# An attention edge stage on one core: products by edge, weighting on DVE, selections on ScalarE

## What is computed

```
ms = src_s[edge_src] + dst_s[edge_dst]           # 64 scalars
mv = src_v[edge_src] + dst_v[edge_dst]           # 32 vectors of 3
w1..w5 = split(h @ rw3 + roff)                   # 224 weights
Y1 = sqrt(3) * edge_vec / |edge_vec|
ds = [w1*ms, w4*(mv . Y1)/sqrt(3)]
dv = [(w2*ms) Y1, w3*mv, w5*cross(mv, Y1)/sqrt(2)]
ls, lv = ds @ lin_ws + lin_bs, einsum(dv, lin_wv)
alpha, vs, vv = ls[:, :64], ls[:, 64:], lv       # 8 heads
a = softmax over the edges of one destination of
    sum_k smooth_leaky(alpha) * alpha_dot
ns = segment_sum(vs * a);  nv = segment_sum(vv * a)
```

## Time and profile before

| | us |
|---|---|
| runs, median of 3 | 9831.51 (9822.02 to 9844.67) |
| the profiled execution | 9813.87 |
| its span | 9812.0 |
| the second edge stage, first to last step on DVE | 5344.8 to 9028.0 |

### The profile page before, as it was taken

How to read it: one execution, slowest core, us unless ns; L and a number is a source line. 1 busy time by engine, 2 the same in 40 slices (tenths; PEclk the granted TensorE clock), 3 DMA queues, 4 the chain that set the end, 5 groups by cost and what they waited for, 6 DMA issues and landing times. The chain is left out here.

```text
span 9812.0 us, 193495 instructions
## 1 busy us (share of the span) xinstructions
PE 8373.1 (85%) x35878; PEld 5079.2 (52%) x35878; DVE 7735.9 (79%) x14864; ACT 4874.4 (50%) x9073; POOL 7372.6 (75%) x4571
## 2 busy tenths in 40 slices
PE   0788888888888869999985999999999999998588
PEld 0444444444444422222222777777777777777233
DVE  3177777777777768888886999999999999998465
ACT  0176666666666631121121555555555555555355
POOL 4378888888888878778774888888888888886331
PEclk9599999999999989999997999999999999999799
DMA  5578888888888877778773666666666666665222
GB/s 208 180 161 167 167 168 166 167 167 167 167 167 167 167 213 275 267 271 282 264 270 109 136 137 144 137 143 137 144 138 144 138 142 137 144 137 122 59 70 52
DMA packets 1235170, 1618.04 MB, mean 165 GB/s; under 512 B 222610, under 2 KB 1010589, under 8 KB 1178973
## 3 DMA queue, kind: packets, MB, share of 16 engines
q1 hardware_dynamic: 758950, 1273.86, 40.0%
q0 software_dynamic: 475584, 338.58, 27.1%
HBM read 1533.79 MB, written 444.07 MB: 202 GB/s over the span
## 5 line engine op out<-in xcount | busy, mean ns | idle before, releaser
L1952 POOL DMA_INDIRECT e_m<-TS,e_at x1568 | 2631.8, 1678 | 583.7 <-issue 461.4
L442 POOL DMA_INDIRECT sums<-e_total,e_place x1568 | 2506.9, 1599 | 565.9 <-DMA sums<-e_total,e_place 314.5
L579 PE MATMUL ps<-e_win,e_pick 128*128 128x448 f32 x3136 | 1325.8, 568 | 165.0 <-DVE e_u L476 97.0
L579 PEld LDWEIGHTS ps<-e_win,e_pick 128*128 128x128 f32 x3136 | 612.5, 201 | 921.6 <-issue 864.1
L2275 ACT ACTIVATE e_dT<-ps 128x512 f32<-128x512 f32 x1176 | 660.0, 596 | 495.5 <-PE ps L2149 340.1
L2275 ACT ACTIVATE e_oT<-ps 128x512 f32<-128x512 f32 x784 | 468.9, 598 | 615.1 <-PE ps L2177 373.2
L742 DVE SCALAR_TENSOR_TENSOR r_y<-ps,w_rb,r_rstd 128x512 f32<-128x512 f32 x394 | 295.6, 750 | 579.9 <-issue 533.2
L1096 POOL TENSOR_TENSOR n_zv<-n_zv,n_ast 128x1536 f32<-128x1536 f32 x200 | 703.6, 3518 | 36.6 <-DMA n_zv<-in_x_groups 22.5
L1936 POOL TENSOR_TENSOR e_val<-e_val 128x640 f32<-128x640 f32 x392 | 670.9, 1712 | 61.9 <-ACT e_val L2252 61.9
L2018 DVE TENSOR_TENSOR e_q<-e_row,dstI 128x512 f32<-128x512 int32 x392 | 704.2, 1796 | 13.3 <-PE ps L2163 13.3
L711 PE MATMUL ps<-r_sq,w_avg 128*128 128x512 f32 x788 | 458.1, 666 | 277.4 <-issue 277.4
(11 more groups left out here) (448 smaller groups left out, 19299.8 us busy)
## 6 DMA issues: line engine op xcount, KB each, us to landing
e_win<-T SPq DMA_DIRECT2D x1568, 168.0 KB
n_z<-in_x_groups SPq DMA_DIRECT2D x400, 512.0 KB
n_zv<-in_x_groups SPq DMA_DIRECT2D x800, 192.0 KB
TOT<-e_tot SPq DMA_DIRECT2D x392, 352.0 KB, 2.6
e_row<-in_src_rows SPq DMA_DIRECT2D x98, 1024.0 KB
e_local<-LR SPq DMA_DIRECT2D x196, 512.0 KB
e_row<-in_dst_rows SPq DMA_DIRECT2D x98, 1024.0 KB
e_win<-TD SPq DMA_DIRECT2D x1568, 60.0 KB
```

Source lines behind the costliest of these rows:

```text
L442: pool.indirect_dma_start(sums[c], bass.IndirectOffsetOnAxis(ap=place[:, r % 4, c:c + 1], axis=0), total[:, r % 4, c, 0:MSG0], None, compu ...
L579: pe.matmul(g[:, c, :], pick[:, p, R * c:R * c + R], win[:, s, c, :], start=True, stop=True).then_inc(spread, 1)
L1952: pool.indirect_dma_start(m_[:, r % 4, c, :], None, TS, bass.IndirectOffsetOnAxis(ap=at[:, gp, col:col + 1], axis=0), compute_op=ALU.add). ...
```

## The change

- **Maps by edge.** `map_scalars` and `map_vectors` take the turned piece as the stationary operand, tile by tile (four products of 128 columns instead of one of 512), so that edges come out on the partitions. The two copies to `oT` and `turn_back` go. Scalars go to bank 4, vectors to bank 5. `map_scalars` waits for ScalarE's `outs` and DVE's `silued` of the step before.
- **Weighting.** `weighted` goes from POOL to DVE, at the beginning of a step, seven behind instead of eight. `totals`, `keep_totals` and `store` go from six to seven behind. `members` is as it was.
- **Selections.** `selections` goes from DVE to ScalarE, as relu(1 - |x - own number|) in two activations.
- **Directions for the heads.** ScalarE repeats `yx` into `ye`, 96 numbers, and one product on DVE with it takes the place of three.
- **Order.** `tops_down` stands before the turns, ScalarE's `results` in the same step, `shift` after `weigh`.

```diff
@@ vector: body
                         more = not (isinstance(t, int) and t == PASSES - 1 and r == STEPS - 1)
+                        if not i.before(7):
+                            weighted(i)
                         if more:
                             sums(after)
                         if r % 4 == 1 and not i.before(5):
                             scans(i)
-                        if i.plus(4).within():
-                            selections(i.plus(4))
                         if not i.before(1):
                             results(i.plus(-1))
+                        if more:
+                            weigh(after)
                         if r % 4 == 1 and not i.before(5):
                             shift(i)
-                        if more:
-                            weigh(after)
                         if not i.before(5):
                             members(i)
@@ vector: results
                     dve.wait_ge(outs, i.n(2, 2))
-                    for x in range(3):
-                        last = dve.tensor_tensor(
-                            turn_by_y[:, :, 4 * x:4 * x + 4].rearrange("r (c h) j -> r c h j", c=GT),
-                            vectors4[:, :, :, 12:16], bc(bc(yx[:, x, bass.ds(i.n(4), GT)], HEADS, 2), 4, 3), ALU.mult)
-                    last.then_inc(by_y, 1)
...
+                    dve.wait_ge(mapped, i.n(2, 2))
+                    y3 = ye[:, p].rearrange("r (c h) i -> r (c h) i", c=GT)
+                    dve.tensor_tensor(turn_by_y[:].rearrange("r a (i j) -> r a i j", i=3),
+                                      bc(vector_out4.rearrange("r c (h x) -> r (c h) x", x=16)[:, :, 12:16], 3, 2),
+                                      bc(y3, 4, 3), ALU.mult).then_inc(by_y, 1)
@@ tensor: totals, map_scalars, map_vectors
-                    j = i.r - 6
+                    j = i.r - 7
...
                     gate(pe, k)
-                    pe.wait_ge(kept, i.n(5, 2))
-                    pe.matmul(ps[:, bank(i, 5), :], W["la"][:].rearrange("u a h x -> u (a h x)"), dT[:, 0, :], start=True, stop=True
-                              ).then_inc(turned, 1)
+                    pe.wait_ge(kept, i.n(3, 1))
+                    if not i.before(1):
+                        gate(pe, k)
+                        pe.wait_ge(outs, i.n(2))
+                        gate(pe, k)
+                        pe.wait_ge(silued, i.n(2, -1))
+                    for c in range(GT):
+                        last = pe.matmul(scalar_out4[:, c], dT[:, 0, R * c:R * c + R],
+                                         W["la"][:].rearrange("u a h x -> u (a h x)"), start=True, stop=True)
+                    last.then_inc(mapped, 1)
...
+                    pe.wait_ge(kept, i.n(3, 3))
+                    if not i.before(1):
                         gate(pe, k)
                         pe.wait_ge(freed, i.n(1))
                     for c in range(GT):
-                        last = pe.transpose(out4[:, c, 128 * j:128 * j + 128], oT[:, j, R * c:R * c + R], I[:])
+                        pe.matmul(vector_out4[:, c], dT[:, 1, R * c:R * c + R], W["lb"][:].rearrange("u h x -> u (h x)"),
+                                  start=True, stop=False)
+                        last = pe.matmul(vector_out4[:, c], dT[:, 2, R * c:R * c + R],
+                                         W["lc"][:].rearrange("u h x -> u (h x)"), start=False, stop=True)
                     last.then_inc(mapped, 1)
@@ scalar: selections
+                    act.activation(pick[:, p, :], local[:, gp, GT * R * s:GT * R * s + GT * R], ACT.Abs, bias=minus[:, 0:1]
+                                   ).then_inc(distant, 1)
+                    gate(act, k)
+                    act.wait_ge(distant, i.n(1, 1))
+                    act.activation(pick[:, p, :], pick[:, p, :], ACT.Relu, bias=one[:, 0:1], scale=-1.0).then_inc(picked, 1)
@@ scalar: body
+                        if r % 4 == 2 and not i.before(6):
+                            weigh_up(i.plus(-1))
                         keep(i, 0)
                         keep(i, 1)
-                        if not i.before(6):
-                            keep_totals(i, 0)
+                        if i.plus(4).within():
+                            selections(i.plus(4))
                         keep(i, 2)
-                        keep(i, 3)
-                        if not i.before(6):
+                        results(i)
+                        if not i.before(7):
+                            keep_totals(i, 0)
                             keep_totals(i, 1)
-                        if r % 4 == 1 and not i.before(5):
-                            weigh_up(i)
-                        keep(i, 4)
```

More of the change, by code:

```diff
@@ L1921, in _ @@
                 passes(sp, body)
-                for r in range(6):
-                    store(At(PASSES, r), 6)
+                for r in range(7):
+                    store(At(PASSES, r), 7)
                 for s in range(STEPS):
@@ L2100, in _ @@
                 dve.wait_ge(ones_set, 2)
-                for r in range(4):
-                    selections(At(0, r))
                 sums(At(0, 0))
@@ L2109, in _ @@
                 for r in range(5):
+                    weighted(At(PASSES, r))
                     members(At(PASSES, r))
+                for r in range(5, 7):
+                    weighted(At(PASSES, r))
             @block.tensor
@@ L2219, in body @@
                         turn(i, 1)
-                        if not i.before(6):
+                        map_scalars(i)
+                        turn(i, 2)
+                        if not i.before(7):
                             totals(i, 0)
-                        turn(i, 2)
-                        if r % 4 == 1 and not i.before(5):
-                            tops_down(i)
-                        map_scalars(i)
-                        if not i.before(6):
+                        map_vectors(i)
+                        if not i.before(7):
                             totals(i, 1)
-                        map_vectors(i)
                         if r % 4 == 0 and not i.before(4):
@@ L2306, in body @@
                             keep_far(i.plus(3), 1, far2(i, 1))
[L2307 to L2308 removed]
+                        if r % 4 == 2 and not i.before(6):
+                            weigh_up(i.plus(-1))
                         keep(i, 0)
                         keep(i, 1)
[L2311 removed]
+                        if i.plus(4).within():
+                            selections(i.plus(4))
+                        keep(i, 2)
+                        results(i)
+                        if not i.before(7):
                             keep_totals(i, 0)
[L2313 to L2315 removed]
                             keep_totals(i, 1)
[L2317 to L2319 removed]
                 act.preload_act_table_set("exp_and_others")
+                act.wait_ge(own_set, 1)
+                for r in range(2):
+                    selections(At(0, r))
                 for r in range(3):
@@ L2324, in _ @@
                         keep_far(At(0, r), half, far2(At(0, 0), half))
+                    if r < 2:
+                        selections(At(0, r + 2))
                 passes(act, body)
-                results(At(PASSES - 1, STEPS - 1))
                 weigh_up(At(PASSES, 1))
-                for r in range(6):
+                for r in range(7):
                     for half in range(2):
```

123 lines of the change are left out of this document (52 added, 71 removed).

## The result

The changed kernel takes **10262.9 us** (median of 4 runs, 10239.0 to 10271.5) beside 9826.8 us for the kernel before on the same chip (4 runs, 9814.6 to 9844.7): a ratio of **1.0438**, 95% interval 1.0413 to 1.0464. It is slower by 436 us, where 243 were forecast: inside the range (9850 to 10300), near its upper end.

A forecast was written before the change was run, and what follows sets the result against it. POOL was taken to bound the kernel before (9.42 us a step), a TensorE-DVE cycle the changed one: 9.35 plus 0.69 for scans is 10.04 us, +243 us over 392 steps, so 10070 us, range 9850 to 10300.

The forecast's parts named there:

- The cycle: Once-a-step ring: TensorE from `map_scalars` to `totals` 4.76 us, DVE from `members` to first result 4.59 us; 9.35 us.
- The step with scans: Every fourth step, `tops_down` ahead of the turns waits for DVE's scans: excess 2.75 us, or 0.69 us a step.
- its upper side: Upper bound of the forecast: TensorE's records at 0.14 instead of 0.11 us add 0.7 us a step, +280 us.
- Hidden terms: TensorE's own chain, the Sync queue's store and the waits for `freed` and `outs` were said to cost nothing.
- TensorE's own chain: TensorE's work from weights to spreads with its short waits in one step, summed to 8.66 us.
- the chain's rival: TensorE's own chain decides if DVE reaches `silued` at least 0.7 us earlier: 8.66 to 8.75 us a step, 9555 us; 12%.
- 5.2 us for the copy against 8 us for the spreads: Sync's store waits for the second totals copy 5.2 us after `map_scalars`; spreads want the windows behind it at 8 us.
- The bound of before: In the kernel before, second edge stage, POOL was called full at 9.42 us a step; DVE only looked full.
- The lock on `e_q`: In the kernel before, DVE's comparison `e_q` sits out POOL's weighting, a mean of 1.1 us a step.
- Weight loads overlap: Rival that TensorE's weight loads don't overlap its products: 2.6 us more in the cycle, 11100 us; 3%.
- `e_q` did not stay long: Rival that indirect DMAs also lock DVE's `e_q`, which stays long: 1.1 us more, 10500 us; 3%.
- The scans did not hide: Rival that the cycle holds but scans and `tops_down` hide in every fourth step: 9.35 us a step, 9805 us; 6%.

The follow-up runs named there:

- e8_store8: The changed kernel with the totals stored eight behind instead of seven, nothing else: 10311.0 us, ratio 1.0490 to the kernel before.
- e6_all: The changed kernel with four buffers of q, `tops_down` behind the third turn and the store eight behind: 9584.1 us, ratio 0.9754 to the kernel before.
- e1_q4: The changed kernel with four buffers of q instead of two, so `members` waits for totals eight behind: 9973.0 us, ratio 1.0142 to the kernel before.
- e3_both: The changed kernel with four buffers of q and `tops_down` moved behind the third turn: 9962.2 us, ratio 1.0137 to the kernel before.
- e10_before_store7: The kernel before with the totals stored seven behind instead of six: 9774.6 us, ratio 0.9964 to the kernel before.

## Why the prediction was right, and what it mis-sized

**The cycle: right.** It is there link by link in the rows above; two edits that cut it each gave 290 us back. Its price was 9.35 us and it takes 9.56 to 9.60: `map_scalars` 0.97 for 0.88 and `map_vectors` 1.88 for 1.76 (the records lie 0.12 apart in the mean; `map_scalars` passes the 0.9 that the prediction had set as the sign that its price was wrong), totals with crossing 0.89 for 0.78, `keep` with crossing 0.65 for 0.75. That is 0.21 x 392 = 82 us.

**The step with scans: the mechanism right, the size not.** Priced at 2.75 us over a plain step, measured 13.37 - 9.56 = 3.81: 1.06 x 98 = 104 us. The term that was missing is the clock. The forecast summed TensorE's links at the price they have at full clock, behind an idle time that it had itself made 3 us long; the two runs with dummy products size that at 0.8 to 1.0 us of the path, of which up to 0.6 us came back in the time. The 82 and the 104 us are nearly all of the 193 us between forecast and result. That 10263 us still lies in the range is in part luck: its upper side was made of records 0.14 us apart, which came out at 0.12, and the clock was in no bound.

**Hidden terms: right only under the cycle.** "Other moves cost nothing while the cycle holds" stands (`e8_store8`), and so does TensorE's own chain: forecast 8.66 us, and from `weights` to `weights` the eight steps of a pass of `e6_all` take 8.68 to 8.98 us in the mean, those with scans too; 9584 us, where the chain's rival had 9555. But that rival was said to need only an earlier `silued`. It also needed the Sync queue: with the cycle cut and the store as it was, 370 to 380 us stayed away (`e1_q4`, `e3_both`). The prediction set 5.2 us for the copy against 8 us for the spreads; it left out the 5 us in which the queue closes its loop, and `load_h` behind the windows.

**The bound of before: half right.** The lock on `e_q` was real, and so was the gain in taking the weighting away. That GpSimd was full at 9.42 us was not: it fits the same work into 9.10 us. VectorE, stopped by the weighting, was as full, and TensorE was overlooked. In the kernel before, four of the eight steps of a pass take it 8.51 to 8.54 us from `weights` to `weights`, in rows without idle time:

```profile
7028.12 1.68 PE L2124 MATMUL ps<-w_r,e_h 128*128 128x224 f32 x8
...
7036.63 1.68 PE L2124 MATMUL ps<-w_r,e_h 128*128 128x224 f32 x8
```

The other four have means from 9.2 to 12.3 us. So the change doesn't shorten TensorE's own chain (8.68 us after); `e6_all` gains by having no long steps. Storing later took the longest from 12.3 to 11.2 us (`e10_before_store7`); what made the rest, no run separates.

**The other rivals.** Weight loads overlap: 24 records and their loads of 128 columns take 2.85 us, no 11100. `e_q` did not stay long. The scans did not hide: 13.1 and 13.6 us, where near 12 was named.

## What to carry to other kernels

When a step is moved further behind, look for every wait that counts by the old distance: a buffer count that was one step of slack can become a ring through the same step, and it shows in the code before it shows in any busy share. Where TensorE is left to wait for about as long as here (3 us), price the work behind the wait at the lower clock too, and ask of each queue that an edit leaves alone whether it could keep up if the edit did all it promises. A part that is worth nothing alone (here the store) can be worth 4% once another limit is gone, so a change that comes out slower is taken apart before it is thrown away.

## What the runs showed of the hardware

- A TensorE idle for 3.05 us came back at a granted clock of 0.50 and stayed there for 5.4 us: 1.91 us for eight turns against 1.04. Two waits of 1.58 and 1.20 us with 1.35 us of products between them did the same (0.52, `weights` 3.27 us against 1.69). Zeros multiplied in the first gap kept the clock at 1.00, and loads that came in time made it worse (0.94 against 0.97 from 5500 to 8700).
- From the branch that closes its loop to its next instruction the Sync queue takes 3.2 us (median of 43 in `e3_both`, 2.7 to 3.4) and issues nothing meanwhile; the same branch costs VectorE, ScalarE and GpSimd 0.05 to 0.23 us there.
- GpSimd's elementwise product stopped a VectorE `tensor_scalar` of 127 elements for 2.0 us (2229 ns in the mean against 0.23 us), though it has one SBUF input.
- GpSimd's indirect DMAs don't stop an instruction with two SBUF inputs: in `e6_all` 285 of 392 `e_q` lie wholly beside one and take 680 ns in the median. A `tensor_scalar` they do hold for a moment: 31 of the 98 masks take 0.35 us in place of 0.23. All of these start 1.2 us into a DMA of 1.55 us and end 0.02 us behind it, as here:

```profile
7201.09 0.34 DVE L2042 TENSOR_SCALAR e_mask<-e_mask 128x127 f32<-128x127 f32 x1
```

```profile
7199.87 1.55 POOL L1944 DMA_INDIRECT e_m<-TS,e_at  x1 [0.30 <-issue]
```
